# Attention projection of a three-layer graph network from float32r halves of features and weights

## The chip, the cores and the metric

One NeuronCore of a Trainium2 chip (trn2) runs the whole program in one launch. The metric is the device time of that core in microseconds (us). TensorE is called PE below, with its weight loads as PEld; VectorE is DVE, ScalarE is ACT, GpSimd is POOL, and SyncE (which only issues DMAs here) is SP.

## The reference

Two graph blocks follow one another. The first is three GATv2 layers over 6250 nodes with 32 features and 106250 edges, sorted by their target node; it holds nearly all that the change touches:

```
xl = (x @ Wl + bl).reshape(n, H, C)            # H = 8 heads, C = 32
xr = (x @ Wr + br).reshape(n, H, C)
e = leaky_relu(xl[src] + xr[dst], 0.2)
logits = einsum('ehc,hc->eh', e, att)
m = segment_max(logits, dst)
p = exp(logits - m[dst]);  denom = segment_sum(p, dst)
alpha = p / (denom[dst] + 1e-16)
out = segment_sum(xl[src] * alpha[:, :, None], dst).mean(heads) + bias
x = batchnorm(leaky_relu(out, 0.01) + x)       # per layer, three times
```

The second is one equivariant convolution (spherical harmonics of the edge vectors, a small radial network, products of gathered node features, a segment sum) between two layer norms. All values are float32.

## The kernel before, in words

**Data.** Nodes lie as `xn[128, 52, 32]` in SBUF (49 blocks of 128 nodes, padded to 52). Edges are cut into steps of 256 (two per partition), each step belonging to one target block: NS = 468 steps per layer. Six steps make a body, eight bodies a group of 48 steps; a layer has ten groups, the last of six bodies. Behind them come 26 self steps (`SELF`), in which nodes play the part of edges to themselves.

**One step of the first pass (logits).** POOL copies two columns of indices (`number`, L484), and issues two indirect gathers (`attention_body`, L503) of 128 rows each from the DRAM tensor `table`, 32 floats a row, into columns 96:128 of `xg`; it also keeps the rows of an earlier step in `xs` (`keep_rows`, L492). SP loads the edges' target places (`load_places`, L424), and DVE makes a one-hot matrix of them (`one_hot_t`, L1193). PE (`front`, L640) transposes the two tiles of `xg` (L646) into the PSUM tile `xt_ps`, which puts the sources' features on partitions 96 to 127, and overwrites partitions 0 to 95 with the targets' features: one bf16 matmul of `x3` with the one-hot (L649). `x3` is `xn` split into three bf16 parts (96 columns), made by five DVE instructions at the start of each layer (L1392 to L1396). ACT copies the tile to SBUF as `xt` (`keep`, L869). Then `zed` (L652) projects it: for each half e of the step, a float32 matmul of `xt` with `wz` (L658, 128 rows: three copies of Wr and one of Wl; 264 columns, of which 256 are the heads' channels and 8 a linear part of the logits) and a bf16 matmul that adds the biases (L660). DVE applies relu and the attention vector (`weighted`, L1198) and sums over channels (`over_channels`, L1206); ACT copies the linear part (L876); once in three steps DVE adds the two (`logits`, L1212).

**One step of the second pass (weights and sums)** belongs to the group before: ACT builds a one-hot matrix (L858, L862), DVE multiplies rows by weights (`weigh_rows`, L1225), PE sums them by target with float32 matmuls (`aggregate`, L673), and DVE adds them into `acc` (`add_sums`, L1239).

**Order.** The engines' programs are written by hand as loops with semaphores. Within step s PE issues front(s+4), aggregate(s) and zed(s+2); DVE issues weigh_rows(s), add_sums(s-2), one_hot_t(s+5), weighted(s), over_channels(s). aggregate(s) waits for add_sums(s-2) (two PSUM tiles); weighted(s) waits for zed(s); POOL may gather six steps ahead of front (`front_done`, six buffers of `xg`). The first group of a layer has only the first pass. Between groups stands the running maximum over segments (`pe_maxima` L696, `maxima` L1307, `running` L1297), a chain that alternates between DVE and PE; PE puts the first fronts and the first two zeds of the next group in its gaps, and POOL's buffers fill meanwhile.

**Start of a layer.** DVE raises `x_new` (L1390). On it SP writes `xn` to `table` (L429, one DMA, rows of 128 bytes lying one after the other, so that a partition's 6272 bytes are one piece) and then queues the loads of target places behind it. POOL waits for the table (`tab_new`, L533) before its first gather. PE waits for `x3_new`.

**Self steps.** ACT copies node rows to `xw` (`self_rows`, L923 and L924), PE transposes them (`self_front`, L731), ACT copies them to `xt` (`self_keep`, L929), then zed, weighted, linear (L876) and over_channels, two steps per loop turn, with nothing beside them: the first self_keep of a turn stands behind the second `linear` of the turn before in ACT's program.

**Memory.** `gate` (softmax gates of a layer's end), `at`, `pg`, `lg` and `px` are idle while the tiles that the change lays over them are in use.

Of the kernel before, what the change touches and what calls it, by code (L numbers as in the profile page):

```python
# [31 lines left out]
P = 128  # L32
N, C, H, LAYERS, E = 6250, 32, 8, 3, 106250
# [37 lines left out]
F32, BF16, I32 = mybir.dt.float32, mybir.dt.bfloat16, mybir.dt.int32  # L71

# [6 lines left out]
def gatv2_program(nc, x, src, dst, edge_w, edge_v, Wl, bl, Wr, br, att, conv_bias, gamma, beta,  # L79
# [3 lines left out]
    with ctx:  # L83
# [10 lines left out]
        table = dram("table", (P * BLOCKS, C))  # L94
# [10 lines left out]
        x3 = sb("x3", [P, NB, 3 * C], BF16)  # L105
# [17 lines left out]
        wz = sb("wz", [P, LAYERS, ZW])  # L123
# [9 lines left out]
        xg = sb("xg", [P, S6, 2, P])  # L133
# [15 lines left out]
        run_f = sb("run_f", [P, CW])  # L149
        run_b = sb("run_b", [P, CW])  # L150
# [17 lines left out]
        at = sb("at", [P, 2, 3 * HC])  # L168
        slope = sb("slope", [P, LAYERS])
# [93 lines left out]
        hid = xt  # L263
        w2e = sb("w2e", [P, 384])
# [58 lines left out]
        x3_new = sem("x3_new")  # L323
# [49 lines left out]
        def _(sp):  # L373
# [3 lines left out]
            for k in range(3):  # L377
                sp.dma_start(wz[32 * k:32 * k + 32, :, 0:HC], Wr.rearrange("l c k -> c l k")).then_inc(s_wt, 16)
            sp.dma_start(wz[96:128, :, 0:HC], Wl.rearrange("l c k -> c l k")).then_inc(s_wt, 16)
# [82 lines left out]
        def _(pool):  # L462
# [25 lines left out]
            def keep_rows(t, to, s):  # L488

                pool.wait_ge(gat[s], 32 * t + 32)  # L490
                then()
                nc.gpsimd.tensor_copy(to, xg[:, s, :, 96:128]).then_inc(xs_done, 1)  # L492
# [35 lines left out]
            with pool.Fori(0, LAYERS) as l:  # L528
# [4 lines left out]
                pool.wait_ge(tab_new, 16 * (l + 1))  # L533
# [59 lines left out]
            pool.wait_ge(tab_new, 16 * (LAYERS + 1))  # L593
# [13 lines left out]
        def _(pe):  # L607
# [32 lines left out]
            def front(l, k, s, t):  # L640

                r = s % 2
                pe.wait_ge(gat[s], 32 * t + 32)
                pe.wait_ge(xt_done, AHEAD + l * ZS + k - 1)
                for e in range(2):
                    pe.transpose(xt_ps(r)[:, e * P:(e + 1) * P], xg[:, s, e, :], ident[:])  # L646
# [106 lines left out]
            with pe.Fori(0, LAYERS) as l:  # L753
                pe.wait_ge(x3_new, l + 1)
# [87 lines left out]
        def _(act):  # L842
# [21 lines left out]
            def keep(l, g, i, k, s):  # L864
# [4 lines left out]
                op.copy(xt[:, r, :], xt_ps(r)[:, 0:PAIR]).then_inc(xt_done, 1)  # L869
# [49 lines left out]
            def self_rows(l, m, r):  # L919
# [3 lines left out]
                op.copy(xw[:, r, :, 0:C], xn[:, pair, :])  # L923
                op.copy(xw[:, r, :, 96:128], xn[:, pair, :]).then_inc(xw_done, 1)  # L924

            def self_keep(l, m, r):
                act.wait_ge(front_done, AHEAD + l * ZS + NS + m + 1)
                act.wait_ge(z_done, AHEAD + l * ZS + NS + m - 1)
                op.copy(xt[:, r, :], xt_ps(r)[:, 0:PAIR]).then_inc(xt_done, 1)  # L929
# [93 lines left out]
        def _(v):  # L1023
# [82 lines left out]
            for w, parts in ((wz[:], P), (bsum.rearrange("p (l z) -> p l z", l=LAYERS), 96)):  # L1106
# [5 lines left out]
            op.tensor_scalar(atts[:].rearrange("p l k -> p (l k)"), watt, 1.0 - NSLOPE, None, ALU.mult)  # L1112

# [183 lines left out]
            def running(l, g):  # L1297
# [6 lines left out]
                op.tensor_tensor_scan(run_f[:], fl[:, 0:CW], lt_ps, -BIG, ALU.add, ALU.max)  # L1304
                op.tensor_tensor_scan(run_b[:, ::-1], fl[:, 1:CW + 1][:, ::-1], lt_ps[:, ::-1], -BIG, ALU.add, ALU.max)

            def maxima(l, g, more):  # L1307
# [16 lines left out]
                op.tensor_tensor(run_f[:], run_f[:], run_b[:], ALU.max)  # L1324
# [6 lines left out]
                op.scalar_tensor_tensor(run_f[:], open_f, carried[:, 0:1], run_f[:], ALU.add, ALU.max)  # L1331
                b = v.value_load(brow[0:1, bass.ds(g * GS, 1)], min_val=0, max_val=BLOCKS - 1)
                seq(None)
                seq(op.scalar_tensor_tensor(run_f[:], open_b, carried[:, 1:2], run_f[:], ALU.add, ALU.max))
# [334 lines left out]
```

## Time and profile before

| | |
|---|---|
| runs of the kernel before | 7020.23, 7012.04, 7016.35 us; median 7016.35 us |
| profiled execution, span from first to last instruction | 7015.3 us |
| its instructions | 173867 |
| busy: PE / PEld / DVE / ACT / POOL | 83% / 61% / 85% / 47% / 69% of the span |
| DMA | 237.88 MB in 214546 packets, mean 34 GB/s |

The profiled execution gives its span alone: no time outside it is listed, and it lies 1.05 us below the median of the runs and inside their spread of 8.19 us. "Busy" is the union of an engine's instructions over the span. The chain of work that ended last assigns 43% of the span to PE, 16% to DVE, 9% to POOL and 17% to issue. The rows of the trace on which the prediction rests follow in a section of their own.

### The profile page before, as it was taken

The page shows a single profiled execution, that of the slowest core. Times are in us where ns is not written, and L with a number is a line of the kernel's source. Part 1 is how long each engine was busy: PE and PEld are TensorE (multiplying, and loading weights), DVE is VectorE, ACT ScalarE, POOL GpSimd, SP SyncE. Part 2 cuts the span into 40 slices and gives each one's busy share as a digit, 9 for nine tenths or more (in the row PEclk, how much of TensorE's full clock was granted, in tenths as well). Part 3 has the DMA queues.
Part 4 walks back from the last instruction along what each step waited for, and adds up shares of the span by engine and source line. Part 5 has one row for each costly group of instructions (what it writes and reads, how often), then busy time and mean ns, then how long its engine had stood idle before and what let it go on. Part 6 is the DMA issues. An engine that isn't in the chain of part 4 may idle for free.

```text
span 7015.3 us, 173867 instructions
## 1 busy us (share of the span) xinstructions
PE 5813.7 (83%) x27916; PEld 4277.5 (61%) x27917; DVE 5946.5 (85%) x12084; ACT 3310.9 (47%) x10977; POOL 4860.6 (69%) x7291
## 2 busy tenths in 40 slices
PE   0589898888579898898757898998864999999998
PEld 0366666665546666666445666666644777777776
DVE  7689999998669999899767999999977888888888
ACT  0155555556125555555513555555541444444444
POOL 1788888783288888788048887888603777777775
PEclk8789999999689999999959999999985999999999
DMA  2211111111011111111001111111201111111111
GB/s 84 64 34 37 36 36 39 34 36 16 6 39 36 36 36 39 34 36 36 7 16 38 36 39 33 37 36 36 34 0 32 34 34 35 34 34 33 34 35 29
DMA packets 214546, 237.88 MB, mean 34 GB/s; under 512 B 72925, under 2 KB 195902, under 8 KB 213950
## 3 DMA queue, kind: packets, MB, share of 16 engines
q1 hardware_dynamic: 93630, 163.53, 7.7%
q0 software_dynamic: 120704, 72.40, 6.7%
q14 instruction: 185, 1.52, 0.1%
q8 instruction: 27, 0.44, 0.0%
HBM read 222.44 MB, written 13.20 MB: 34 GB/s over the span
## 4 chain that ended last, share of the span: by engine, by line
PE 43%; issue 17%; DVE 16%; DVEq 9%; POOL 9%; DMA 3%; POOLq 1%; ACT 1%; ACTq 0%; SPq 0%
PE psum L673 16%; PE psum L658 12%; PE psum L804 3%; PE psum L660 3%; POOL xg L558 3%; DVEq L1232 3%; PE psum L646 2%; POOL xg L503 2%; PE psum L818 2%; DMA xg<-table,idx 2%; DVE u L1198 2%; DVE acc L1239 2%; DVEq L1028 1%; DVE xs L1573 1%; PE psum L649 1%
## 5 line engine op out<-in xcount | busy, mean ns | idle before, releaser
L503 POOL DMA_INDIRECT xg<-table,idx x2808 | 2885.2, 1028 | 712.3 <-PE psum L649 250.7
L658 PE MATMUL psum<-wz,xt 128*128 x5928 | 1823.3, 401 | 49.8 <-ACT xt L929 49.7
L673 PE MATMUL psum<-px,oh 128*128 128x272 f32 x5616 | 1643.6, 417 | 255.9 <-DVE acc L1239 240.7
L673 PEld LDWEIGHTS psum<-px,oh 128*128 128x128 f32 x5616 | 961.0, 191 | 650.0 <-DVE acc L1239 433.8
L658 PEld LDWEIGHTS psum<-wz,xt 128*128 128x128 f32 x5928 | 1001.5, 197 | 406.9 <-issue 65.4
L1198 DVE SCALAR_TENSOR_TENSOR u<-psum,atts 128x512 f32<-128x512 f32 x1482 | 1012.3, 683 | 220.1 <-PE psum L660 219.4
L558 POOL DMA_INDIRECT xg<-table,idx x936 | 902.2, 964 | 394.0 <-issue 219.6
L1206 DVE TENSOR_REDUCE lr<-u 128x16 f32<-128x512 f32 x1482 | 1012.3, 685 | 107.7 <-DVE u L1198 58.9
L1225 DVE TENSOR_TENSOR px<-xs,pg 128x528 f32 (+1 forms) x1404 | 991.0, 706 | 80.1 <-PE psum L673 40.2
L858 ACT ACTIVATE dist<-iota_f,ndloc 128x128 f32<-128x128 f32 x2808 | 974.3, 394 | 95.0 <-PE psum L673 72.1
L876 ACT COPY lin<-psum 128x16 f32<-128x16 f32 x1482 | 254.7, 172 | 1284.2 <-DVE u L1198 1283.4
L869 ACT COPY xt<-psum 128x256 f32<-128x256 f32 x1404 | 522.4, 372 | 691.7 <-PE psum L660 383.3
L804 PE MATMUL psum<-w2e,xt 128*128 128x384 f32 x1872 | 723.5, 510 | 145.5 <-ACT xt L979 83.4
L660 PE MATMUL psum<-bz,ones_b 96*128 x2964 | 839.9, 283 | 0.0
L818 PEld LDWEIGHTS psum<-xs,oh 128*128 128x128 f32 x3744 | 626.5, 191 | 173.1 <-issue 51.4
L646 PE MATMUL psum<-ident,xg 128*128 128x128 f32 x2808 | 580.5, 290 | 182.5 <-DMA xg<-table,idx 174.5
L818 PE MATMUL psum<-xs,oh 128*128 128x192 f32 x3744 | 704.9, 332 | 6.4 <-DVE acc L1591 2.5
L1239 DVE TENSOR_TENSOR acc<-acc,psum 128x272 f32 x1404 | 606.2, 432 | 77.1 <-issue 30.3
L646 PEld LDWEIGHTS psum<-ident,xg 128*128 128x128 f32 x2808 | 373.1, 150 | 387.4 <-issue 201.6
L862 ACT ACTIVATE oh<-dist 128x256 f32<-128x256 f32 x1404 | 585.4, 417 | 44.3
L516 POOL TENSOR_TENSOR xp<-xn,gate 128x512 f32 (+1 forms) x78 | 89.6, 1151 | 631.9 <-DVEq L1028 497.1
L804 PEld LDWEIGHTS psum<-w2e,xt 128*128 128x128 f32 x1872 | 320.9, 191 | 298.7 <-issue 122.4
(273 smaller groups left out, 7330.2 us busy)
## 6 DMA issues: line engine op xcount, KB each, us to landing
dr<-dlocs SPq DMA_DIRECT2D x468, 192.0 KB
xg<-table,idx POOLq DMA_INDIRECT x3744, 2.4
at<-w_rows SPq DMA_DIRECT2D x156, 192.0 KB, 3.1
fl<-flags SPq DMA_DIRECT2D x30, 576.2 KB
flags<-fl SPq DMA_DIRECT2D x10, 576.2 KB, 3.2
table<-xn SPq DMA_DIRECT2D x3, 784.0 KB, 3.8
xp<-keys SPq DMA_DIRECT2D x5, 385.0 KB, 4.4
u<-keys SPq DMA_DIRECT2D x5, 385.0 KB, 4.4
```

What stands on the lines that cost most here:

```text
L503: nc.gpsimd.indirect_dma_start(out=xg[:, s % S6, t, 96:128], out_offset=None, in_=table, in_offset=bass.IndirectOffsetOnAxis(ap=idx[:, s, ...
L558: nc.gpsimd.indirect_dma_start(out=feat[:, s, e, 8:8 + WIDE], out_offset=None, in_=table1, in_offset=bass.IndirectOffsetOnAxis(ap=idx[:, s ...
L646: pe.transpose(xt_ps(r)[:, e * P:(e + 1) * P], xg[:, s, e, :], ident[:])
L658: pe.matmul(out_z, xt[:, r, e * P:(e + 1) * P], wz[:, bass.ds(l, 1), :].rearrange("p o z -> p (o z)"), start=True, stop=False)
L660: last = pe.matmul(out_z, ones_b[:], bz[:, bass.ds(l, 1), :].rearrange("p o z -> p (o z)"), start=False, stop=True)
L673: last = pe.matmul(agg_ps(r), oh[:, s % 3, e, :], px[:, s % 3, e, :], start=(e == 0), stop=(e == 1))
L804: last = pe.matmul(psum[:, 2 * r + e, 0:HC + P], rows, w2e[:], start=True, stop=True)
L818: pe.matmul(parts[:, 0:24, 0:8], oh[:, r, e, :], prod[:, :, 8 * h:8 * h + 8], start=(e == 0 and h == 0), stop=(e == 1 and h == 1))
L858: last = op.activation(dist[:, e, :], iota_f[:], ACT.Abs, bias=ndloc[:, bass.ds(k, 1), e])
L1198: op.scalar_tensor_tensor(u[:, r], z_ps(r, 0, HC), 0.0, atts[:, bass.ds(l, 1), :].to_broadcast([P, 2, HC]), ALU.max, ALU.mult).then_inc(u_ ...
L1206: op.tensor_reduce(lr[:, c, j], u[:, r].rearrange("p e (h c) -> p e h c", h=H), AX.X, ALU.add).then_inc(r_done, 1)
L1225: op.tensor_tensor(px[:, r, :, 0:H * C1].rearrange("p e (h c) -> p e h c", h=H), rows.unsqueeze(2).to_broadcast([P, 2, H, C1]), pg[:, 2 * ...
```

## The change

The three bf16 parts of the features give way to two float32r halves: `hn` becomes the float32r rounding of `xn`, and `x_lo` (laid over `gate`) the rest. The weights get the same split, `wz_hi` and `wz_lo`. A tile of 128 partitions now holds target-high, target-low, source-high, source-low, and is multiplied once by `wz_hi` (rows Wr, Wr, Wl, Wl) and once by `wz_lo`: four partial products in two float32r matmuls where one float32 matmul stood. `table` rows grow from 32 to 96 floats (high, low, exact), written by three DMAs that each fill a third of every row; a gather brings all 96 (384 bytes). The targets' halves are selected with two bf16 matmuls of 64 columns each (`x4`, two bf16 parts per half) instead of one of 96. The semaphore `hl_new` lets SP start the table once the two halves exist. Some tiles are laid over idle ones.

```diff
-        table = dram("table", (P * BLOCKS, C))
+        table = dram("table", (P * BLOCKS, 3 * C))
-        xg = sb("xg", [P, S6, 2, P])
+        xg = sb("xg", [P, S6, 2, P + C])
...
-                sp.wait_ge(x_new, l + 1)
-                sp.dma_start(table.rearrange("(p b) c -> p b c", p=P), xn[:, 0:BLOCKS, :]).then_inc(tab_new, 16)
+                sp.wait_ge(hl_new, l + 1)
+                for k, part in enumerate((hn[:], x_lo, xn[:])):
+                    sp.dma_start(table.rearrange("(p b) c -> p b c", p=P)[:, :, k * C:(k + 1) * C], part[:, 0:BLOCKS, :]).then_inc(tab_new, 16)
...
-                            out=xg[:, s % S6, t, 96:128], out_offset=None, in_=table,
+                            out=xg[:, s % S6, t, 2 * C:5 * C], out_offset=None, in_=table,
...
-                pool.wait_ge(tab_new, 16 * (l + 1))
+                pool.wait_ge(tab_new, 48 * (l + 1))
...
-                pe.matmul(xt_ps(r)[0:96, 0:PAIR], x3[:, bass.ds(b, 1), :].rearrange("p o c -> p (o c)"),
-                          oht[:, s, :], start=True, stop=True).then_inc(front_done, 1)
+                for part in range(2):
+                    last = pe.matmul(xt_ps(r)[0:2 * C, 0:PAIR], x4[:, bass.ds(b, 1), part, :].rearrange("p o c -> p (o c)"),
+                                     oht[:, s, :], start=(part == 0), stop=(part == 1))
+                last.then_inc(front_done, 1)
...
-                    pe.matmul(out_z, xt[:, r, e * P:(e + 1) * P], wz[:, bass.ds(l, 1), :].rearrange("p o z -> p (o z)"),
+                    rows = xt[:, r, e * P:(e + 1) * P].bitcast(F32R)
+                    pe.matmul(out_z, rows, wz_hi[:, bass.ds(l, 1), :].rearrange("p o z -> p (o z)").bitcast(F32R),
                               start=True, stop=False)
+                    pe.matmul(out_z, rows, wz_lo[:, bass.ds(l, 1), :].rearrange("p o z -> p (o z)").bitcast(F32R),
+                              start=False, stop=False)
                     last = pe.matmul(out_z, ones_b[:], bz[:, bass.ds(l, 1), :].rearrange("p o z -> p (o z)"),
...
-                op.copy(xw[:, r, :, 0:C], xn[:, pair, :])
-                op.copy(xw[:, r, :, 96:128], xn[:, pair, :]).then_inc(xw_done, 1)
+                twice = xw[:, r].rearrange("p e (q t c) -> p t e q c", q=2, t=2)
+                op.copy(twice[:, 0], hn[:, pair, :].unsqueeze(2).to_broadcast([P, 2, 2, C]))
+                op.copy(twice[:, 1], x_lo[:, pair, :].unsqueeze(2).to_broadcast([P, 2, 2, C])).then_inc(xw_done, 1)
...
+            seq(op.tensor_copy(wz_hi[:].bitcast(F32R), wz_raw))
+            seq(op.tensor_tensor(wz_lo[:].bitcast(F32R), wz_raw, wz_hi[:], ALU.subtract))
...
-                seq(op.tensor_copy(x3[:, :, 0:C], xn[:]))
-                seq(op.tensor_tensor(hn[:], xn[:], x3[:, :, 0:C], ALU.subtract))
-                seq(op.tensor_copy(x3[:, :, C:2 * C], hn[:]))
-                seq(op.tensor_tensor(hn[:], hn[:], x3[:, :, C:2 * C], ALU.subtract))
-                seq(op.tensor_copy(x3[:, :, 2 * C:3 * C], hn[:]))
-                v.sem_inc(x3_new, 1)
+                seq(op.tensor_copy(hn[:].bitcast(F32R), xn[:]))
+                seq(op.tensor_tensor(x_lo, xn[:], hn[:], ALU.subtract))
+                v.sem_inc(hl_new, 1)
+                op.tensor_copy(x4[:, :, 0, 0:C], hn[:])
+                seq(op.tensor_copy(x4[:, :, 0, C:2 * C], x_lo))
+                op.tensor_tensor(x4[:, :, 1, 0:C], hn[:], x4[:, :, 0, 0:C], ALU.subtract)
+                seq(op.tensor_tensor(x4[:, :, 1, C:2 * C], x_lo, x4[:, :, 0, C:2 * C], ALU.subtract))
+                v.sem_inc(x4_new, 1)
...
```

ACT's two copies into `xt` write it as float32r. The tiles `run_f` and `run_b` move over `at`, `hid` over `pg`, `w2e` over `lg`, and the raw weights over `px`; no instruction is added by that.

## Rows read from the trace of the kernel before

**Rows 1.** The page: shares of the chain that ended last, by engine.

```profile
PE 43%; issue 17%; DVE 16%; DVEq 9%; POOL 9%; DMA 3%; POOLq 1%; ACT 1%; ACTq 0%; SPq 0%
```

**Rows 2.** Windows: start:end, length, busy us and instructions per engine, clock share, DMA.

```profile
1924.00:2088.00 164.00, 109.21 (x473) 66.05 (x474) 101.10 (x204) 31.57 (x110) 140.28 (x227) 0.85 0.19 43
2555.00:2655.00 100.00, 93.26 (x464) 67.28 (x464) 90.78 (x191) 60.39 (x215) 88.26 (x143) 1.00 0.17 41
3450.00:3515.00 65.00, 43.63 (x228) 30.42 (x228) 43.67 (x93) 23.98 (x116) 0.00 (x0) 1.00 0.00 0
```

**Rows 3.** Timeline: start, us, engine, line, operation [idle before]; DVE and PE in one step.

```profile
2603.93 0.68 DVE L1198 SCALAR_TENSOR_TENSOR u<-psum,atts 128x512 f32<-128x512 f32 x1
2604.15 1.18 PE L673 MATMUL psum<-px,oh 128*128 128x272 f32 x4
2605.17 0.61 PE L658 MATMUL psum<-wz,xt 128*128 x2
2605.61 0.28 PE L660 MATMUL psum<-bz,ones_b 96*128 x1
2605.73 0.61 PE L658 MATMUL psum<-wz,xt 128*128 x2
2606.53 0.68 DVE L1198 SCALAR_TENSOR_TENSOR u<-psum,atts 128x512 f32<-128x512 f32 x1
```

**Rows 4.** Line L1198, 2090 to 3460 us: count, then what it waited for (us, times).

```profile
L1198 DVE SCALAR_TENSOR_TENSOR u<-psum,atts x420: 675/683/692, 2091.6 to 3459.0; 128x512 f32<-128x512 f32 x140
  PE psum L660: 2.1, 2
```

**Rows 5.** Line L503, 2088 to 3280 us, in the same form, and its time to landing.

```profile
L503 POOL DMA_INDIRECT xg<-table,idx x773: 977/981/1704, 2088.2 to 3280.0; - x194
  PE psum L649: 82.4, 11
```

**Rows 6.** Line L503 in a layer's first group, 1929 to 2088 us: all its waits.

```profile
L503 POOL DMA_INDIRECT xg<-table,idx x114: 951/981/2444, 1929.8 to 2086.8; - x114
  issue: 11.6, 49
  POOL idx L484: 8.5, 53
  POOL xs L492: 1.9, 12
```

**Rows 7.** Timeline of a later layer's start.

```profile
1924.87 0.33 SPq L429 DMA_DIRECT2D table<-xn  x1
1926.05 1.89 DVE L1393 TENSOR_TENSOR hn<-xn,x 128x1664 f32<-128x1664 f32 x1
1929.79 2.44 POOL L503 DMA_INDIRECT xg<-table,idx  x1 [3.66 <-issue]
```

**Rows 8.** DMA issues of the page: the table write, KB, us to landing.

```profile
table<-xn SPq DMA_DIRECT2D x3, 784.0 KB, 3.8
```

**Rows 9.** Timeline of the first layer's start.

```profile
205.10 0.33 SPq L429 DMA_DIRECT2D table<-xn  x1
219.22 1.07 POOL L503 DMA_INDIRECT xg<-table,idx  x1 [0.67 <-POOL idx L484]
```

**Rows 10.** DMA view, 12.0 to 12.5 us: packets of the 128-byte pieces of `wn`.

```profile
DMA packets 516, 0.07 MB, mean 139 GB/s; under 512 B 516, under 2 KB 516, under 8 KB 516
```

**Rows 11.** DMA view, 104.5 to 105.25 us: 512-byte pieces written to `dlocs` in DRAM.

```profile
DMA packets 432, 0.22 MB, mean 298 GB/s; under 512 B 12, under 2 KB 432, under 8 KB 432
```

**Rows 12.** Timeline of one turn of the self steps.

```profile
3465.03 0.71 PE L658 MATMUL psum<-wz,xt 128*128 x2 [1.36 <-ACT xt L929]
3467.66 0.69 DVE L1198 SCALAR_TENSOR_TENSOR u<-psum,atts 128x512 f32<-128x512 f32 x1 [0.43 <-PE psum L660]
3468.83 0.37 ACT L929 COPY xt<-psum 128x256 f32<-128x256 f32 x1 [0.27 <-issue]
```

**Rows 13.** Line L558, gathers of 192-byte rows: count, ns min/median/max.

```profile
L558 POOL DMA_INDIRECT xg<-table,idx x936: 949/955/1023, 5387.5 to 6973.4; - x188
```

More of the change, by code:

```diff
@@ L71 @@
 F32, BF16, I32 = mybir.dt.float32, mybir.dt.bfloat16, mybir.dt.int32
+F32R = mybir.dt.float32r
 def steps_of(l, g, i, s):
@@ L104, in gatv2_program @@
         hn = sb("hn", [P, NB, C])
-        x3 = sb("x3", [P, NB, 3 * C], BF16)
+        x4 = sb("x4", [P, NB, 2, 2 * C], BF16)
         acc = sb("acc", [P, NB, AGG])
@@ L121, in gatv2_program @@
         ones_b = sb("ones_b", [96, P], BF16)
-        wz = sb("wz", [P, LAYERS, ZW])
+        wz_hi = sb("wz_hi", [P, LAYERS, ZW])
+        wz_lo = sb("wz_lo", [P, LAYERS, ZW])
         bz = sb("bz", [96, LAYERS, ZW], BF16)
@@ L148, in gatv2_program @@
         fl = sb("fl", [P, 3 * CW + 1], BF16)
-        run_f = sb("run_f", [P, CW])
-        run_b = sb("run_b", [P, CW])
         ends = sb("ends", [P, 4, CH])
@@ L168, in gatv2_program @@
         at = sb("at", [P, 2, 3 * HC])
+        run_f, run_b = at[:, 0, :], at[:, 1, :]
+        x_lo = gate[:].rearrange("p a b c -> p (a b c)").rearrange("p (b c) -> p b c", c=C)
         slope = sb("slope", [P, LAYERS])
@@ L262, in gatv2_program @@
         pa = u[:]
-        hid = xt
-        w2e = sb("w2e", [P, 384])
+        hid = pg[:].rearrange("p k c h -> p (k c h)")[:, 0:2 * PAIR].rearrange("p (r e) -> p r e", r=2)
+        wz_raw = px[:].rearrange("p a b c -> p (a b c)")[:, 0:LAYERS * ZW].rearrange("p (l z) -> p l z", l=LAYERS)
+        w2e = lg[:].rearrange("p k c h -> p (k c h)")[:, 0:384]
         pb = xs[:].rearrange("p a b c d -> p (a b c d)")[:, 0:S6 * 768].rearrange("p (a e i x) -> p a e i x", a=S6, e=2, i=3)
@@ L322, in gatv2_program @@
         x_new = sem("x_new")
-        x3_new = sem("x3_new")
+        x4_new = sem("x4_new")
+        hl_new = sem("hl_new")
         tab_new = sem("tab_new")
@@ L375, in _ @@
             sp.dma_start(xn[:, 0:BLOCKS, :], x).then_inc(s_in, 16)
-            for k in range(3):
-                sp.dma_start(wz[32 * k:32 * k + 32, :, 0:HC], Wr.rearrange("l c k -> c l k")).then_inc(s_wt, 16)
-            sp.dma_start(wz[96:128, :, 0:HC], Wl.rearrange("l c k -> c l k")).then_inc(s_wt, 16)
+            for k, w in enumerate((Wr, Wr, Wl, Wl)):
+                sp.dma_start(wz_raw[32 * k:32 * k + 32, :, 0:HC], w.rearrange("l c k -> c l k")).then_inc(s_wt, 16)
             sp.dma_start(watt, att.rearrange("l h c -> (l h c)").partition_broadcast(P)).then_inc(s_wt, 16)
@@ L491, in keep_rows @@
                 then()
-                nc.gpsimd.tensor_copy(to, xg[:, s, :, 96:128]).then_inc(xs_done, 1)
+                nc.gpsimd.tensor_copy(to, xg[:, s, :, P:P + C]).then_inc(xs_done, 1)
             def attention_body(l, i, starts):
@@ L591, in gathers1 @@
                     gather1(k + s, 3 * half + s)
-            pool.wait_ge(tab_new, 16 * (LAYERS + 1))
+            pool.wait_ge(tab_new, 48 * LAYERS + 16)
             pool.wait_ge(l1_go, 1)
@@ L645, in front @@
                 for e in range(2):
-                    pe.transpose(xt_ps(r)[:, e * P:(e + 1) * P], xg[:, s, e, :], ident[:])
+                    pe.transpose(xt_ps(r)[:, e * P:(e + 1) * P], xg[:, s, e, 0:P], ident[:])
                 b = pe.value_load(brow[0:1, bass.ds(k, 1)], min_val=0, max_val=BLOCKS - 1)
                 pe.wait_ge(oht_done, AHEAD + l * NS + k + 1)
-                pe.matmul(xt_ps(r)[0:96, 0:PAIR], x3[:, bass.ds(b, 1), :].rearrange("p o c -> p (o c)"),
-                          oht[:, s, :], start=True, stop=True).then_inc(front_done, 1)
+                for part in range(2):
+                    last = pe.matmul(xt_ps(r)[0:2 * C, 0:PAIR], x4[:, bass.ds(b, 1), part, :].rearrange("p o c -> p (o c)"),
+                                     oht[:, s, :], start=(part == 0), stop=(part == 1))
+                last.then_inc(front_done, 1)
             def zed(l, n, r):
@@ L753, in _ @@
             with pe.Fori(0, LAYERS) as l:
-                pe.wait_ge(x3_new, l + 1)
+                pe.wait_ge(x4_new, l + 1)
                 early_fronts(l, 0, (0, 1, 2, 3))
@@ L868, in keep @@
                 act.wait_ge(z_done, AHEAD + l * ZS + k - 1)
-                op.copy(xt[:, r, :], xt_ps(r)[:, 0:PAIR]).then_inc(xt_done, 1)
+                op.copy(xt[:, r, :].bitcast(F32R), xt_ps(r)[:, 0:PAIR]).then_inc(xt_done, 1)
             def linear(l, n, r, q, c, j):
@@ L928, in self_keep @@
                 act.wait_ge(z_done, AHEAD + l * ZS + NS + m - 1)
-                op.copy(xt[:, r, :], xt_ps(r)[:, 0:PAIR]).then_inc(xt_done, 1)
+                op.copy(xt[:, r, :].bitcast(F32R), xt_ps(r)[:, 0:PAIR]).then_inc(xt_done, 1)
             with act.Fori(0, LAYERS) as l:
@@ L1105, in _ @@
                                  bsum2.rearrange("p (l z) -> p l z", l=LAYERS)[0:96, :, 0:HC], ALU.add))
-            for w, parts in ((wz[:], P), (bsum.rearrange("p (l z) -> p l z", l=LAYERS), 96)):
+            for w, parts in ((wz_raw, P), (bsum.rearrange("p (l z) -> p l z", l=LAYERS), 96)):
                 seq(op.tensor_tensor(wtmp[0:parts].rearrange("p (l k) -> p l k", l=LAYERS), w[0:parts, :, 0:HC],
@@ L1303, in running @@
                 v.wait_ge(c_lt, q + 1)
-                op.tensor_tensor_scan(run_f[:], fl[:, 0:CW], lt_ps, -BIG, ALU.add, ALU.max)
+                op.tensor_tensor_scan(run_f, fl[:, 0:CW], lt_ps, -BIG, ALU.add, ALU.max)
                 op.tensor_tensor_scan(run_b[:, ::-1], fl[:, 1:CW + 1][:, ::-1], lt_ps[:, ::-1], -BIG, ALU.add, ALU.max)
@@ L1323, in maxima @@
                 v.sem_inc(c_car, 1)
-                op.tensor_tensor(run_f[:], run_f[:], run_b[:], ALU.max)
+                op.tensor_tensor(run_f, run_f, run_b, ALU.max)
                 op.tensor_scalar(fix[:, 0:1], open_f[0:H, 0:1], 0.0, None, ALU.is_ge)
@@ L1330, in maxima @@
                 seq(op.tensor_reduce(carried[:], back[:], AX.X, ALU.add))
-                op.scalar_tensor_tensor(run_f[:], open_f, carried[:, 0:1], run_f[:], ALU.add, ALU.max)
+                op.scalar_tensor_tensor(run_f, open_f, carried[:, 0:1], run_f, ALU.add, ALU.max)
                 b = v.value_load(brow[0:1, bass.ds(g * GS, 1)], min_val=0, max_val=BLOCKS - 1)
                 seq(None)
-                seq(op.scalar_tensor_tensor(run_f[:], open_b, carried[:, 1:2], run_f[:], ALU.add, ALU.max))
+                seq(op.scalar_tensor_tensor(run_f, open_b, carried[:, 1:2], run_f, ALU.add, ALU.max))
                 v.sem_inc(c_t, 1)
```

## The prediction, as put on record before the run

> **What bounds the kernel now.** I read the page's shares of the chain first: PE has 43%, more than any other engine [rows 1]. A change that shortens PE's work looks well aimed by that, but shares are an average over stages, so the next view is the windows, and in them the line that takes what PE's projection makes.
>
> In a full group PE is busy 93.26 of 100 us, DVE 90.78 and POOL 88.26, at clock share 1.00 [rows 2]. Which one sets the pace is told by who waits. DVE's `weighted` (L1198) is the only consumer of zed's 256 columns. In 420 executions, nine groups and more, it waited for PE 2.1 us in all [rows 4]. DVE's step runs back to back: L1198 starts at 2603.93 and again at 2606.53, 2.60 us, in which no gap before it is listed [rows 3]. PE is as full only because DVE hands it each aggregate late: zed is issued two steps ahead, so its result lies ready. The change removes nothing from DVE's step. POOL is behind by little: it waited 82.4 us for PE in 11 pauses, about one per group, between 2088 and 3280 us [rows 5]; these are the running maxima. So full groups are bound by DVE.
>
> In a layer's first group there is only the first pass. POOL waits for nobody there: its three kinds of idle time are its own issue and index copies, 22.0 us, and none is for PE [rows 6]; it is busy 140.28 of 164 us [rows 2]. It is the bound, and a first gather that starts later shifts the whole layer. The self steps are the third stage: PE is busy 43.63 of 65 us there, yet DVE waits for it and PE waits for ACT [rows 2, 12], a closed chain in which zed's length counts in full.
>
> **PE's part.** A float32 matmul is two records (x2 at L658). They hold 0.44 us (2605.61 less 2605.17), 0.22 each; the bf16 matmul of the same 264 columns holds 0.12 us (2605.73 less 2605.61) [rows 3]. One e costs 0.56 us. No row shows a float32r matmul. Bounds: 0.11 to 0.12 us, as the bf16 pass, or 0.22, as one float32 record. I take 0.12, nearest in that one matmul would be one pass, and get 3 x 0.12 = 0.36 instead of 0.56 per e, 0.2 to 0.22 less; 0.44 less per step with two e. `front` has one more bf16 pass of 256 columns, +0.11. Net -0.33 us on PE in each of 1404 steps, -463 us of PE work. In full groups this lies beside DVE's step: worth 0. If the upper bound holds, zed costs what it did and PE's step is 0.11 longer; PE's own step was 2.6 of DVE's 2.60, so up to 0.05 us on 1200 steps, 60 us, would show.
>
> In the running maxima one more pass per early front stands before three PE instructions of the chain, each of which has a DVE instruction of 0.1 us or more still running when it is due; 0 to +0.2 us in 27 of them, 0 to 5 us, taken 2.
>
> Self steps: a turn issues two zeds, from 3465.03 to before 3467.66, where DVE's second L1198 waited 0.43 us for them; ACT's next copy follows at 3468.83 [rows 12]. Two zeds are 4 e, 4 x 0.22 = 0.88 us less per turn, 13 turns in each of 3 layers: -34 us at most, 0 if float32r is not cheaper. ACT's four copies per turn go from 64 to 128 columns, with over a microsecond until PE needs them: 0. But PE, busy 67% there at full clock, would be busy less; and in the first groups, at 109.21 of 164 us, its granted share is 0.85 [rows 2]. So part of the gain may be lost to the lower level of 1.2 GHz: at it the four e take 4 x 0.72 us, more than the 4 x 0.56 of now. Taken: -20 us. The last zeds of a first group, for which DVE waits after POOL's last gather: -1 us a layer, -3.
>
> **The table's part.** Before, one DMA of 128 pieces lands 3.8 us after its issue at 1924.87; POOL's first gather is at 1929.79 and is stretched to 2.44 us beside DVE's splitting, against 0.98 [rows 5, 7, 8]. Now SP waits for one copy and one subtract on DVE: the same two as before end at 1926.05 + 1.89 = 1927.94 [rows 7], so the issue is at 1928.0, +3.1 us. Then come three DMAs. Each moves 49 x 128 = 6272 pieces of 128 bytes, since a piece of a row ends every 32 floats in DRAM: 18816 pieces against 128. No row shows such a write. The nearest ones: 128-byte pieces of a load ran at 516 in 0.5 us, 0.97 ns each [rows 10]; 512-byte pieces written to DRAM ran at 432 in 0.75 us, 1.74 ns each [rows 11]. I take 1.5 ns, nearer the second because it is a write: 28.2 us. The bounds give 18.2 and 32.7. To this comes what is not transfer in the 3.8 us; about 2.2 us of it is the 784 KB, so 1.6.
>
> Later layers (two): landing at 1928.0 + 29.8 = 1957.8 instead of 1928.7, +29.1; less 1.46 for the stretched gather, +27.7 (17.7 to 32.2). First layer: POOL clears `acc` until 217.5 and gathers at 219.22, while the table was issued at 205.10 [rows 9], so about 10 us are covered. Landing at 205.1 + 29.8 = 234.9, gather 0.7 later, +16.4 (6 to 21). Sum 2 x 27.7 + 16.4 = 71.8 us (42 to 85). The loads of target places queue behind the table on SP's ring, but land soon after it and are needed only with the first front. The rest of DVE's splitting (`x4`, four instructions in place of three) runs beside the write: 0. POOL's issue of a gather would be dear if it grew with the row's width, since POOL binds the first groups and is next in the others. Rows of 128 bytes take 981 ns at the median [rows 5], rows of 192 bytes in the second block 955 [rows 13]: it doesn't grow, 0 for 384. Two instructions more on DVE in the setup (some 1.7 us) lie beside POOL's loads.
>
> The Trainium skill (DMA: Bandwidth & Descriptors, Specifications) says that DMAs need pieces of at least 512 bytes for full rate, and that below this the engine does a read-modify-write. No row here shows a write below 512 bytes of any number.
>
> **Sum.** 7015.3 + 71.8 - 20 - 3 + 2 = 7066 us. The medians of the runs lie 1 us above this execution's span: 7067. This measurement tells a change from none at about 0.2%, 14 us.
>
> **Rivals.**
> *A, small writes are read and written back.* Each 128-byte piece costs a read and a write of DRAM, two slots at 1.74 ns: 3.5 ns, 65.5 us a layer, 37 more than taken: +37 x 3 = 112, 7179 us. For: it is a write of a part of what memory keeps together. Against: only loads of that size are seen, and these are quick. This is the mechanism that the skill's sentence names, and it speaks against the change. Chance 0.13.
> *B, PE loses its clock.* PE's work per step falls from 2.6 to 2.27 of 2.8 us, nearer to the first groups (0.85) than to 1.00 [rows 2]. At half clock a step holds twice 2.0 or so, 4.0 us, 1.2 longer than the pace; two or three such steps per full group cost 3 us, 27 times: +80, 7147. Against: it then is busy throughout and regains the clock. Chance 0.12.
> *C, faster.* The full groups do gain: an earlier zed and aggregate take DVE's gaps at the loop turns. It decides only if DVE's step waits for PE, and [rows 4] say no. The cap is POOL's slack, 82.4 us over 8 groups, 10.3 each [rows 5], 278 us over 27; half of it: 7066 - 139 = 6927. Chance 0.1.
> *D, the table is cheap.* The pieces go at 0.97 ns, and the self steps keep all 34 us: 7015.3 + 42 - 34 - 3 + 0 = 7020. Chance 0.1.
> *E, float32r costs two records' time*, the change doesn't do what it says: self steps gain 0, full groups lose up to 60: 7067 + 20 + 3 + 20 to 60, 7110 to 7150. Chance 0.05.
>
> **How the numbers follow.** The forecast has 0.5. Its own range is 7030 to 7095, by the bounds of the write (42 to 85) and of the self steps (0 to -34). The overall range takes in D, B, E and A and leaves out C and the tails: 7005 to 7185. Faster by over 0.2% is C, 0.1, and a fifth of D and of the forecast's fast tail, 0.04 together: 0.14. Within 0.2%: most of D and a little of the forecast, 0.12. Slower: 0.74.
>
> **What would show it.** L1198 in full groups still waits for PE for almost nothing and a group still lasts 148 us; PE's busy share there falls to some 80%. Between SP's first table DMA and POOL's first gather lie some 30 us in the later layers. L658's two instructions are single records 0.12 us apart. A turn of the self steps lasts 0.5 to 0.9 us less. Full groups of under 146 us would prove me wrong about DVE, a table that lands within 12 us about the write, and L658 records of 0.22 us about float32r.

## The result, and the profile after

The changed kernel takes 7063.2 us (median of four runs, 7056.58 to 7073.68) against 7016.2 of the kernel before in the same series. The ratio is estimated at 1.0069, with a 95% interval of 1.0054 to 1.0083. A second series gave 1.0075 (1.0059 to 1.0092). It is slower, and near the 7067 us forecast, but its parts are not those forecast. The profiled execution has a span of 7054.8 us, 39.5 more than before.

The first three groups of rows answer to [rows 2, 4, 5]: windows of a first group, a full group and the self steps, then the two lines that the argument hung on.

```profile
1950.00:2107.00 157.00, 116.34 (x521) 75.45 (x522) 92.31 (x195) 30.49 (x107) 135.72 (x223) 0.71 0.26 61
2450.00:2550.00 100.00, 82.74 (x443) 59.76 (x442) 90.36 (x190) 52.17 (x186) 78.83 (x125) 0.95 0.22 55
3475.00:3530.00 55.00, 37.13 (x239) 28.11 (x237) 43.00 (x90) 30.65 (x129) 0.00 (x0) 1.00 0.00 0
```

```profile
L1210 DVE SCALAR_TENSOR_TENSOR u<-psum,atts x419: 676/684/692, 2109.8 to 3397.9; 128x512 f32<-128x512 f32 x140
  PE psum L669: 1.0, 2
```

```profile
L507 POOL DMA_INDIRECT xg<-table,idx x767: 976/981/1707, 2107.9 to 3299.5; - x192
  PE psum L654: 88.8, 23
```

PE is relieved as forecast (82.74 of 100 us in place of 93.26), `weighted` still waits for it for nothing (1.0 us in 419), and a gather of 384 bytes a row takes POOL the same 981 ns. The granted share of the clock is lower too: 0.71 in the first group in place of 0.85, and 0.95 in a full group in place of 1.00.

One step of PE, which answers to [rows 3]: the four `zed` matmuls of `wz_hi` and `wz_lo` are single records.

```profile
2477.43 0.37 PE L665 MATMUL psum<-wz_hi,xt 128*128 x1
2477.64 0.28 PE L667 MATMUL psum<-wz_lo,xt 128*128 x1
2477.76 0.29 PE L669 MATMUL psum<-bz,ones_b 96*128 x1
2477.89 0.39 PE L650 MATMUL psum<-ident,xg 128*128 128x128 f32 x2
```

The three starts of an e are not evenly spaced. From L667 to L669 it is 0.12 us, as taken; from L665 to L667 it is 0.21 (the median of all 763 pairs between 2111 and 3300 us, and of those in the self steps), and the L665 of a second e follows only 0.04 behind the L669 of the first. So an e repeats after 0.37 us (3487.13, 3487.50 in the self steps), against 0.56 before. An e with another instruction behind it, as here, takes 0.46 (2477.43 to 2477.89).

The start of a later layer answers to [rows 7].

```profile
1928.71 1.03 DVE L1404 CAST hn<-xn 128x1664 fp32r<-128x1664 f32 x1 [3.12 <-issue]
1931.10 1.89 DVE L1405 TENSOR_TENSOR gate<-xn,hn 128x1664 f32<-128x1664 f32 x1 [1.37 <-issue]
1933.05 0.55 SPq L433 DMA_DIRECT2D table<-hn  x1
1933.65 3.80 SPq L433 DMA_DIRECT2D table<-gate  x1
1937.50 5.39 SPq L433 DMA_DIRECT2D table<-xn  x1
1950.19 1.02 POOL L507 DMA_INDIRECT xg<-table,idx  x1 [20.29 <-issue]
```

And half a microsecond of that write, in the view of the DMA queues:

```profile
DMA packets 641, 0.08 MB, mean 164 GB/s; under 512 B 641, under 2 KB 641, under 8 KB 641
```

From the first table DMA to the first gather are 17.1 us; a piece of 128 bytes goes by in 0.5/641 us = 0.78 ns, with the 16 DMA engines at least 90% busy in every slice of that view. The first layer answers to [rows 9]: the clearing of `acc` still covers most, and the gather moved by 3.1 us.

```profile
204.96 0.58 SPq L433 DMA_DIRECT2D table<-hn  x1
222.30 0.99 POOL L507 DMA_INDIRECT xg<-table,idx  x1 [4.33 <-issue]
```

Cutting both traces at the same marks (DVE's first instruction of a layer, the first gather, the start of the `weighted` that opens each group and of the first and the last one of the self steps) gives this ledger, in us, before to after:

```
                         layer 1            layer 2            layer 3            sum
start to first gather    17.6 -> 21.3       4.8 -> 21.5       4.9 -> 21.4       +36.8
first group             157.6 -> 156.7    156.9 -> 157.4     157.1 -> 158.5       +1.1
eight full groups      1186.6 -> 1196.3  1186.3 -> 1195.6   1186.0 -> 1196.4     +29.5
last group              185.5 -> 185.5    184.9 -> 184.7     183.8 -> 184.5       +0.4
self steps               52.7 -> 43.0      52.7 -> 43.1      52.7 -> 43.2       -28.6
all the rest                                                                      +0.3
```

Forecast were +71.8 for the first line, -20 for the self steps, -3 for the first groups, +2 for the maxima, and 0 for the full groups. The 29.5 us of the full groups were not foreseen. Experiments were chosen for them and for the write.

### The profile page after: what moved, and what is told of

Its sections match the earlier page's. It is cut to its first block and busy times, and to the rows that moved or that the text cites. A ratio compares the mean times of both kernels' runs of the same rounds, so it can differ in the third digit from the quotient of the medians.

```text
span 7054.8 us, 178164 instructions
## 1 busy us (share of the span) xinstructions
PE 5748.6 (81%) x29320; PEld 4248.1 (60%) x29321; DVE 5985.6 (85%) x12089; ACT 3321.1 (47%) x10977; POOL 4884.6 (69%) x7291
## 5 line engine op out<-in xcount | busy, mean ns | idle before, releaser
L682 PE MATMUL psum<-px,oh 128*128 128x272 f32 x5616 | 1674.5, 423 | 326.9 <-DVE acc L1251 248.4
L665 PE MATMUL psum<-wz_hi,xt 128*128 x2964 | 1286.9, 434 | 50.1 <-ACT xt L939 49.8
L669 PE MATMUL psum<-bz,ones_b 96*128 x2964 | 896.0, 302 | 0.0
L667 PE MATMUL psum<-wz_lo,xt 128*128 x2964 | 875.9, 296 | 0.0
L878 ACT CAST xt<-psum 128x256 fp32r<-128x256 f32 x1404 | 522.3, 372 | 717.5 <-PE psum L669 394.5
L813 PE MATMUL psum<-lg,pg 128*128 128x384 f32 x1872 | 722.9, 510 | 154.2 <-ACT pg L989 99.8
L650 PE MATMUL psum<-ident,xg 128*128 128x128 f32 x2808 | 599.5, 298 | 212.8 <-DMA xg<-table,idx 207.9
L665 PEld LDWEIGHTS psum<-wz_hi,xt 128*128 128x128 f32 x2964 | 618.0, 209 | 172.9 <-ACT lin L885 58.4
L654 PE MATMUL psum<-oht,x 128*64 128x256 bf16 x2808 | 636.8, 309 | 83.7 <-issue 62.9
L1251 DVE TENSOR_TENSOR acc<-acc,psum 128x272 f32 x1404 | 606.7, 432 | 79.6 <-issue 29.5
L667 PEld LDWEIGHTS psum<-wz_lo,xt 128*128 128x128 f32 x2964 | 609.4, 206 | 40.1
```

The costliest lines, as they stand in the source:

```text
L665: pe.matmul(out_z, rows, wz_hi[:, bass.ds(l, 1), :].rearrange("p o z -> p (o z)").bitcast(F32R), start=True, stop=False)
L667: pe.matmul(out_z, rows, wz_lo[:, bass.ds(l, 1), :].rearrange("p o z -> p (o z)").bitcast(F32R), start=False, stop=False)
L682: last = pe.matmul(agg_ps(r), oh[:, s % 3, e, :], px[:, s % 3, e, :], start=(e == 0), stop=(e == 1))
L813: last = pe.matmul(psum[:, 2 * r + e, 0:HC + P], rows, w2e[:], start=True, stop=True)
```

## The experiments

All times are medians beside runs of the kernel before on the same chip (7012 us in the first two series, 7014 and 7013 in the last two).

**Only the wide gather and its table.** Two kernels, one from either side.

```
-  sp.dma_start(table..., xn[:, 0:BLOCKS, :])                    # wide_before
+  for k, part in enumerate((xn[:], xn[:], xn[:])):
+      sp.dma_start(table...[:, :, k * C:(k + 1) * C], part[:, 0:BLOCKS, :])
-  out=xg[:, s % S6, t, 96:128]
+  out=xg[:, s % S6, t, 2 * C:5 * C]

-  for k, part in enumerate((hn[:], x_lo, xn[:])): sp.dma_start(table...)     # narrow_after
+  sp.dma_start(table.rearrange("(p b) c -> p b c", p=P), xn[:, 0:BLOCKS, :])
-  out=xg[:, s % S6, t, 2 * C:5 * C]
+  out=xg[:, s % S6, t, 4 * C:5 * C]
```

> The kernel before, but with the table of 96 floats a row (the same features three times), written by three DMAs of 6272 pieces each, and with the wide gather; PE's, ACT's and DVE's work is that of before, and so is the result. Theory W (write and wide gather are the two costs): 7016 + 31 + 30 = 7077 us, a full group at 149.4. Rival X (the gather's width costs nothing in the groups): 7016 + 31 = 7047 us, a full group at 148.2. My recorded price of the write (+71.8 us) would give 7088 or more with groups at 148.2.

> The changed kernel, but the table keeps only the 32 exact floats of a row: it is written by one DMA of 128 long pieces as before, and a gather brings 128 bytes in place of 384 (the features of source rows do not enter the projection; all instructions of PE, ACT and DVE stay). Theory W (the write of the table costs about 36 us of the 47, and the full groups' +1.2 us each comes from the wider gather): 7063 - 30 - 30 = 7003 us, a full group back at 148.2. Rival X (the groups' part comes from PE's second front matmul or the moved tiles): 7063 - 30 = 7033 us, a full group still 149.4. In both the first gather of a later layer comes 8 us after the layer's first cast in place of 21.5.

wide_before: 7039.9 us, +28.0 (ratio 1.0040, 1.0026 to 1.0054). Its full groups last 148.3 us, as before; the first gather comes 17.2 and 17.4 us after a later layer's start in place of 4.8 and 4.9, and 20.5 in place of 17.6 in the first: 27.8 us, which is all of it. narrow_after: 7033.2 us (1.0030, 1.0018 to 1.0042), 27 under the changed kernel's 1.0069, and its groups stay at 148.5 to 150.5. Theory W falls: the width of the gather costs the groups nothing. Of the 36.8 us, 28 are the write, and the other 9 the wait for `hn` and `x_lo`, which the write now stands behind. narrow_after shows this wait alone: its first gather comes 9.1 and 9.0 us after a later layer's start, 4.2 more than before, and 0.1 more in the first layer.

**Long pieces.** The same bytes in 384 pieces instead of 18816:

```
-  table.rearrange("(p b) c -> p b c", p=P)[:, :, k * C:(k + 1) * C], part[:, 0:BLOCKS, :]
+  table.rearrange("(k p b) c -> k p (b c)", k=1, p=P)[0, :, k * BLOCKS * C:(k + 1) * BLOCKS * C], part[:, 0:BLOCKS, :]...
```

> The changed kernel with the same three table DMAs and bytes, but each written as 128 pieces of 6272 bytes in place of 6272 pieces of 128 bytes; the rows of the table are then not the rows that the gathers mean, so the features of the source rows are wrong, and nothing else changes. Theory N (the number of pieces makes the write long): by the 3.8 us of one such DMA before, 3 x 2.2 + 1.6 = 8 us instead of 17 from the first issue to the first gather, in each later layer 9 us less, in the first 3 less: 7063 - 21 = 7042 us. Rival B (the bytes make it long): 7063 us.

7041.4 us (1.0046, 1.0029 to 1.0063), as theory N said. From the first DMA to the first gather are now 9.0 us:

```profile
1929.11 0.33 SPq L433 DMA_DIRECT2D table<-hn  x1
1929.49 0.43 SPq L433 DMA_DIRECT2D table<-gate  x1
1929.96 0.93 SPq L433 DMA_DIRECT2D table<-xn  x1
```

```profile
1938.08 1.03 POOL L507 DMA_INDIRECT xg<-table,idx  x1 [12.12 <-issue]
```

SP's own issue falls too, from 3.80 and 5.39 us to 0.43 and 0.93. So the number of pieces costs 8 us of the 17 in a later layer. Of the other 9, 4.9 were there before, with a third of the bytes in one DMA; 4 come with three times the bytes in three DMAs.

**The tiles that moved, and `front`'s second pass.**

```
-  run_f = sb("run_f", [P, CW])                      # moved_before
-  run_b = sb("run_b", [P, CW])
+  run_f, run_b = at[:, 0, :], at[:, 1, :]

-  for part in range(2):                             # one_x4
+  for part in range(1):
```

> The kernel before, with only the two running-maximum tiles laid over the tile at, as in the change. Theory W: 7016 us. Rival Z (the place of these tiles costs the full groups 1.2 us each): 7016 + 30 = 7046 us.

> The changed kernel without the second matmul of front (the low bf16 parts of the target rows are left out of the projection). Theory W: 7063 us, a full group at 149.4, since PE is not what the groups wait for. Rival X (PE's extra pass delays the logits or the aggregate): 7063 - 30 = 7033 us, a full group at 148.2.

moved_before: 7013.4 us (1.0002, 0.9992 to 1.0012); the place of the tiles is free. one_x4: 7043.4 us (1.0046, 1.0029 to 1.0063), some 17 under the changed kernel, which neither side had said: its full groups last 149.1 us in the mean, so 0.8 each remain with the second pass gone. Part of the 17 us shows below, where the long groups are told.

**Where in a group.** A full group is a first body, a loop of six turns and a last body. Laid step on step, a turn (six steps) takes 16.89 us before and 17.01 after (medians of 144 turns each), and the whole difference sits at one spot, between the second step's `over_channels` and the third step's `weigh_rows`. DVE before, then after:

```profile
2602.17 0.69 DVE L1206 TENSOR_REDUCE lr<-u 128x16 f32<-128x512 f32 x1
2602.78 0.70 DVE L1225 TENSOR_TENSOR px<-xs,pg 128x528 f32 x1
```

```profile
2476.64 0.69 DVE L1218 TENSOR_REDUCE lr<-u 128x16 f32<-128x512 f32 x1
2477.35 0.71 DVE L1237 TENSOR_TENSOR px<-xs,pg 128x528 f32 x1
```

0.61 us from start to start became 0.71. The aggregate that `weigh_rows` has to wait for is that of three steps earlier, long done, and so is POOL's copy (at 2475.90). The records of DVE's sequencer show a pause there: between two neighbouring register instructions lie 0.17 us where 0.05 is usual. Before there is one such pause per turn too, four records later in the step, just behind the issue of `weigh_rows`, under the 0.70 us of which it costs nothing. The changed kernel has four more records of DVE ahead of this loop, three instructions and a semaphore. So both pauses are at the same place of the program. In the loop's first turn the pause is 0.40 us long and stands ahead of the 1097th of all records of DVE and its sequencer, in either kernel. If that is the cause, the number of instructions ahead decides:

```
+  for k in range(3):            # 6 in pad6_after
+      op.memset(filler[:, k:k + 1], 0.0)
   with v.Fori(0, LAYERS) as l:
```

> The kernel before with three one-element memsets of a spare tile on DVE ahead of the loop over layers; nothing reads them, and each takes under 0.1 us once. Theory P: DVE's sequencer pauses 0.12 us more at one fixed place of its program, in every turn of a full group's body; in the kernel before that pause falls behind the issue of weigh_rows (L1225, third step), where it is covered, in the changed kernel three instructions earlier in the step, ahead of that issue. Three instructions more shift it to the same place here: a turn of the body goes from 16.89 to 17.01 us, a full group from 148.3 to 149.0, the whole to 7012 + 27 x 6 x 0.115 = 7031 us. Rival Q (the delay in the changed kernel comes from PE's or ACT's new work): 7012 us, turns at 16.89.

> The changed kernel with six such memsets on DVE ahead of the loop over layers. Theory P: the pause moves six instructions earlier in the step, behind the issue of the tensor_reduce, where the sequencer waits for the engine anyway: a turn back from 17.01 to 16.89 us, a full group from 149.5 to 148.8, the whole 7063 - 19 = 7044 us. Rival Q: 7063 us, turns at 17.01.

Three memsets made the kernel before slower, 7026.9 us (1.0020, 1.0010 to 1.0030), and six made the changed one faster, 7023.4 (1.0016 times the kernel before, 1.0007 to 1.0026). The turn is 17.01 and 16.89 us, as theory P said to the hundredth, and in the loop's first turn the pause stands ahead of record 1097 in both, as it does in self_halves below. The same two lines, in pad3_before and in pad6_after:

```profile
2607.26 0.69 DVE L1207 TENSOR_REDUCE lr<-u 128x16 f32<-128x512 f32 x1
2607.94 0.71 DVE L1226 TENSOR_TENSOR px<-xs,pg 128x528 f32 x1
```

```profile
2611.07 0.69 DVE L1219 TENSOR_REDUCE lr<-u 128x16 f32<-128x512 f32 x1
2611.68 0.70 DVE L1238 TENSOR_TENSOR px<-xs,pg 128x528 f32 x1
```

pad3_before's 24 full groups of the ledger are 14.6 us longer, which is its whole 14.4. pad6_after gained more than the 19 us expected, some 37. Of them 24.7 are in the full groups, where a usual one goes from 149.2 us back to the 148.3 of the kernel before, and six are longer in place of nine (below). Body by body the two runs agree: from the first body on, the place is worth 0.88 us a group in pad3_before and 0.90 in pad6_after. pad3_before also takes 0.25 us off a group's first body, so that 0.63 are left of it. Another 9 us of pad6_after are at the starts and ends of the layers, whose code moved by six instructions too; why those gain was not tried. So 37 of the changed kernel's 48 us go with six instructions that do nothing. What the sequencer does in the pause stays open.

**What is left in the groups.** In the changed kernel 8 of the 24 full groups last 150.0 to 150.5 us, the others 148.5 to 149.5.

> The changed kernel with the six memsets on DVE and without front's second matmul (the low bf16 parts of the target rows are left out of the projection). Theory L: what the full groups lose beside the pause is PE's lower clock at their start; with the six memsets five of 24 full groups lasted 149.3 to 149.5 us in place of 148.2, and these were among those with over 18 us at the lower level. With less to do for PE in the low stretch no group is above 148.8, 5 x 1.1 = 6 us, and some 3 us more at the layers' ends: 7023 - 9 = 7014 us. Rival M (the long groups have nothing to do with PE's work in the low stretch): they stay, and the time is 7020 us or more.

> The changed kernel as it is, beside the same runs of the kernel before. Theory: 7059 us (1.0069 times the kernel before), 36 us above the version with six memsets; its full groups fall into one kind at 149.1 and one at 150.0 to 150.5 us by the length of the lower clock at their start (under 15 us and over 18 us), as in the first profile. Rival: the kinds were chance, and the lengths don't go with the clock.

(The lengths of the lower clock in these two texts were summed over a whole group and set 10 us late. Counted from 0.6 us ahead of the start of the group's first `weighted`, they are up to 3.6 us in the short kind and 5.9 to 6.5 in the long. With the six memsets it was six groups, not five.) after_again: 7068.4 us. 17 of its 24 groups have the long stretch, and apart from the last full group of a layer, which is 0.4 to 0.8 shorter in every kernel, each of these is at 149.88 or above and every other one under 149.5; with eight such groups more (17 against 9), its profile is 11 us longer than the first, 7 of it in the full groups. The windows show the clock in a short and a long group of the first profile (start:end, length, busy us and instructions of PE, PEld, DVE, ACT, POOL, clock, DMA):

```profile
2405.20:2408.70 3.50, 3.50 (x16) 2.42 (x15) 3.36 (x8) 3.21 (x13) 3.14 (x5) 0.66 0.33 76
2408.70:2411.20 2.50, 2.50 (x17) 1.84 (x16) 2.46 (x6) 1.69 (x7) 2.16 (x5) 1.00 0.23 54
3002.80:3006.30 3.50, 3.50 (x13) 2.33 (x12) 3.36 (x8) 2.87 (x11) 3.08 (x5) 0.50 0.35 84
3006.30:3008.80 2.50, 2.50 (x12) 1.68 (x11) 1.96 (x5) 0.68 (x3) 2.17 (x4) 0.60 0.20 43
```

0.50 is the lower of TensorE's two levels, 1.2 GHz, 1.00 the upper, 2.4 GHz. In the short group the full clock is there in the third step; in the long one PE, busy throughout, is still at the lower, and DVE runs dry. Second, third and fourth `weighted` of either:

```profile
2407.97 0.68 DVE L1210 SCALAR_TENSOR_TENSOR u<-psum,atts 128x512 f32<-128x512 f32 x1
2410.45 0.69 DVE L1210 SCALAR_TENSOR_TENSOR u<-psum,atts 128x512 f32<-128x512 f32 x1
2413.12 0.68 DVE L1210 SCALAR_TENSOR_TENSOR u<-psum,atts 128x512 f32<-128x512 f32 x1
```

```profile
3004.97 0.69 DVE L1210 SCALAR_TENSOR_TENSOR u<-psum,atts 128x512 f32<-128x512 f32 x1
3008.21 0.69 DVE L1210 SCALAR_TENSOR_TENSOR u<-psum,atts 128x512 f32<-128x512 f32 x1 [0.50 <-PE psum L669]
3010.92 0.69 DVE L1210 SCALAR_TENSOR_TENSOR u<-psum,atts 128x512 f32<-128x512 f32 x1
```

5.15 us against 5.95. In the mean of the first profile, last groups of a layer aside, the long groups lag behind the short by 0 at the second step, 0.75 at the fourth and 0.95 from the fifth on, so the whole of it is lost in these steps. In the kernel before no full group has more than 3.4 us of the lower clock past its first step. pad6_one_x4 (both edits above) took 7021.3 us (1.0010, 1.0001 to 1.0020), 4 less than pad6_after and not 9: nine of its groups have a stretch of over 5 us, but none is above 148.95. With one pass fewer a late clock costs 0.6 us and not 1.0. one_x4 shows the same: its long groups are 0.4 us over its usual ones, which with 6 long groups in place of 9 is most of the 9.4 us that its full groups gained. Theory L holds for the place and not for the size.

**Filling PE's pauses.** 22 passes of 248 columns in each block of maxima:

```
+  def filler_passes(l, n):
+      for k in range(n):
+          pe.matmul(psum[:, 2, ZW:512], ones_b[:], bz[:, bass.ds(l, 1), 0:512 - ZW]..., start=True, stop=True)
```

> The changed kernel with 22 more bf16 matmuls of 248 columns on PE in each block of running maxima (16 where PE waits 4.4 us for the ends, 6 where it waits 1.8 us for the running maximum); they write columns of PSUM that nobody reads. Theory L (the groups of 150 us are those in which PE's lower clock lasts 6 us past the group's first step, and PE's pauses in the maxima are what keeps it low): with the pauses filled the lower clock ends at most 4 us past the first step in every group, or is not granted at all in the maxima; no group over 149.5 us, 8 to 17 groups x 1.0 us less, 7063 - 12 = 7051 us, and less still if the chain of maxima itself runs at the full clock. Rival M (the long groups have another cause): they stay, and the time is 7063 us or more.

> The same 22 matmuls in each block of maxima in the version that has the halves in the self steps only (6989 us). Theory L: its groups have no long kind (the lower clock ends 3.2 us past the first step at most), so nothing is gained there: 6989 us, unless the clock no longer falls in the maxima, in which case their PE instructions (six transposes of 0.22 us, two zeds and four fronts) take half as long: 1 to 2 us a block, 27 blocks, 6989 - 40 = 6950 us at best. Rival: the filler delays the instructions behind it on PE, 27 x 0.5 us: 7002 us.

fill_after: 7064.4 us (1.0072, 1.0055 to 1.0088), nothing gained. The clock fell 3.5 us later in a block, but rose no earlier: 18 groups have it low for over 6 us. fill_self: 6989.7 us, as without. In the 20 us ahead of a group PE was busy 14.7 us in the mean in place of 11.8, so this fills about a third of its pauses there, and that third is not what makes the clock rise late. A chain with all of them filled was not tried. That it rises late goes with every long group in both profiles of the changed kernel and in those of pad6_after, narrow_after and fill_after; what makes it rise late stays open. It isn't the only thing that lengthens a group: one_x4 has one of 149.58 us whose clock rose early.

**The change in the self steps alone.** `hn`, `x_lo`, `wz_hi`, `wz_lo` for the self steps, everything of the kernel before in the groups:

```
+  for i, w in enumerate((wz_hi, wz_lo) if halves else (wz,)):
+      rows, w = (xr if halves else xt)[:, r, e * P:(e + 1) * P], w[:, bass.ds(l, 1), :]...
```

> The kernel before with the change in the self steps alone: hn and x_lo are made at the layer's start, self_rows and self_keep are those of the changed kernel, zed multiplies wz_hi and wz_lo there; the groups keep the float32 wz, x3, the narrow table and the narrow gather. By the parts as measured (self steps -8.3 us a layer, table and full groups 0): 7012 - 25 = 6987 us, a self turn 3.55 us in place of 4.31. Rival: the two more DVE instructions at the layer's start (2.9 us) delay the first group, 7012 - 25 + 9 = 6996 us. Seven instructions more stand ahead of the body of a full group on DVE; by theory P the pause then falls where it is covered, and groups stay at 148.3.

6988.9 us, 0.9967 times the kernel before (0.9955 to 0.9980), the fastest with fill_self, which is the same but for the filler. The self steps take 44.1 us in place of 52.7, full groups 148.1, and the pause is covered.

## Why the prediction was right, and where not

**What bounds the kernel: right.** DVE sets the full groups, POOL the first ones, the chain of PE, DVE and ACT the self steps. Freeing PE by 10 of 100 us won nothing in a full group.

**The write: the term was mis-sized.** +71.8 was taken, 36.8 came, under the lower bound of 42. The mechanism (pieces, and the wait for DVE) was right. The term that failed is the price of a piece: 1.5 ns was taken, 0.78 measured, less than either row that I bounded it with (0.97 and 1.74). I had chosen the row that was a write over the row that had the size. The wait for DVE was too small, +3.1 taken against 4.2 (narrow_after). The Trainium skill (DMA: Bandwidth & Descriptors, Specifications) has a read-modify-write below 512 bytes; whatever happens inside, these pieces go by faster than the 512-byte ones of [rows 11] (0.78 against 1.74 ns), and rival A's 3.5 ns is out. That small pieces run below the full rate the traces do show: 164 GB/s against the 298 of [rows 11], and 17.1 us to the first gather against the 9.0 of long_pieces for the same bytes. The first layer's term was 16.4 and came as 3.7 for the same reason, since a shorter write is covered there for the most part.

**Full groups, 0: failed.** The step was right that nothing waits for PE in the steady state, and wrong to take from this that the group's length can't change. Two things made up the 29.5 us. The larger is the place of DVE's program: the pause of its sequencer came into the open, and with six idle instructions the usual full group is back at the 148.3 us of the kernel before, so that 24.7 us of the 29.5 are gone. No term of the sum stood for it. The smaller is rival B's mechanism: nine groups are about 1.0 us longer than the usual ones, 9 us in all, and the six that are left in pad6_after make up the 4.7 us that its full groups are over those before. B priced it at 3 us in each of 27 groups; it came as 1 us, at the third to fifth step of a third of them.

**The self steps: right in kind, -28.6 and not -20.** A turn went from 4.31 to 3.55 us and lost 0.76 of the 0.88, four times the 0.19 us of an e. I had held back 14 us for a lower clock; the granted share is 1.00 in the window above with PE busy 68% of the time, as before.

**float32r: right on the path.** Each float32r matmul is one record, and an e fell from 0.56 to 0.37 us, near the 0.36 taken; where another instruction follows it is 0.46, and in the groups either is worth nothing. The sign that was named did not come as written: L665 and L667 are 0.21 us apart and not 0.12, near the 0.22 that was to prove me wrong, and the time comes back in the 0.04 ahead of the next e. The repeat of a whole e decides, and by it rival E is out, for the self steps gained. C is out too: no full group is under 148.5 us. D had the write nearly right and the total wrong.

The total came out within 4 us because the errors cancel: -35 in the write and -9 in the self steps against +29.5 in the full groups and +4 in the first ones. That is luck. (The profiled execution is the fastest of the four; these parts add up to 39.5 us there, and the medians lie 47 apart.) The forecast deserves credit for its sign, not for its closeness.

## What to carry to other kernels

A bottleneck engine that waits for nobody can still get slower when its own program is shifted: if a loop that the change does not touch changes by a tenth of a microsecond per turn, compare the same turn step by step, and try a few idle instructions ahead of it before blaming the change. Put a faster form only where the engine it frees is waited for: here the self steps, which gave 8.6 us a layer by themselves and 9.5 in the whole change, and nothing else. And when a DMA is cut into small pieces, price it by the number of pieces, in SP's issue and in the transfer.

## Unexpected in the hardware

- DVE's sequencer pauses 0.12 us more at one instruction of a loop body of 131 records, in every turn. The pause keeps its place in the program (ahead of record 1097) while the code moves: three instructions more ahead bring it into the open in one kernel, six cover it in the other.
- Pieces of 128 bytes go from SBUF to DRAM at 0.78 ns each, and SP takes 3.8 to 5.4 us to issue the second and third DMA of 6272 of them, against 0.3 to 0.9 for a DMA of 128 pieces.
- TensorE's full clock comes back either up to 3.6 us or about 6 us past a group's start, nothing between in the two profiles of the changed kernel, and 3 us more of PE's work in the 20 us ahead of it did not bring it earlier.
- A gather's issue on POOL costs 981 ns for rows of 128 and of 384 bytes.
- Of two float32r matmuls and a bf16 one, all of 264 columns, the starts are 0.21, 0.12 and 0.04 us apart, and the three repeat after 0.37 us.
